# Two DVE operations of 512 columns in an edge loop, each made as two of 256

## The reference

```python
edge_attr = swish(edge_attr_raw @ enc_W + enc_b)
for _ in range(4):
    e_in = concatenate([edge_attr, x[src], x[dst]], axis=-1)
    e_upd = layernorm(swish(e_in @ eW1 + eb1) @ eW2 + eb2, eg, ebeta)
    edge_attr = edge_attr + e_upd
    agg = segment_sum(edge_attr, dst, 3125)
    n_in = concatenate([x, agg], axis=-1)
    x = x + layernorm(swish(n_in @ nW1 + nb1) @ nW2 + nb2, ng, nbeta)
```

## Time and profile before

| | |
|---|---|
| three runs | 3330.44, 3335.55 (median), 3336.2 us |
| the profiled execution | 3340.0 us, its span 3338.2 us |
| busy share of the span | PE 78%, DVE 70%, ACT 62%, POOL 51% |
| mean granted TensorE clock | 0.944 of full speed |

### The profile page before, as it was taken

One profiled execution on the slowest core, in us unless ns is written; L12 is line 12 of the kernel. 1 busy time (PEld: TensorE's weight loads), 2 busy tenths in 40 slices (PEclk: granted clock), 3 DMA queues, 4 the chain that ended last, 5 costly groups with the idle time before them and its releaser, 6 DMA issues.

```text
span 3338.2 us, 86010 instructions
## 1 busy us (share of the span) xinstructions
PE 2607.4 (78%) x28086; PEld 1912.4 (57%) x28086; DVE 2346.5 (70%) x6798; ACT 2072.7 (62%) x5534; POOL 1707.8 (51%) x1679
## 2 busy tenths in 40 slices
PE   3665888888886788888887788888888688888885
PEld 1332666666663566666664566666665466666664
DVE  6884677777784577777775477777776377777778
ACT  3774666666663666666664566666664466666672
POOL 1445565656522555555530656665640656666640
PEclk8666999999998999999998899999999799999998
DMA  4776566666644566666653566666653455555540
GB/s 129 247 240 211 171 197 195 196 199 196 194 138 130 164 197 193 196 197 193 195 159 114 155 199 195 203 195 197 198 168 112 143 156 160 157 161 157 163 135 23
DMA packets 492917, 578.04 MB, mean 173 GB/s; under 512 B 82399, under 2 KB 341724, under 8 KB 492446
## 3 DMA queue, kind: packets, MB, share of 16 engines
q1 hardware_dynamic: 417198, 366.82, 34.6%
q0 software_dynamic: 75264, 205.62, 23.0%
HBM read 428.62 MB, written 144.35 MB: 172 GB/s over the span
## 4 chain that ended last, share of the span: by engine, by line
PE 54%; issue 17%; ACT 10%; DVE 7%; another core or an unknown queue 6%; DMA 3%; SPq 1%; DVEq 1%; ACTq 0%; POOL 0%; POOLq 0%
PE psum L1137 12%; PE psum L1153 12%; PE psum L1129 11%; PE psum L1121 4%; PE psum L1101 4%; PE psum L1169 4%; ACT arena L1267 3%; ACT arena L1255 3%; ACT psum L1241 2%; DMA arena<-attr_p 2%; PE psum L1148 2%; PE psum L1566 2%; PE psum L1605 1%; ACT arena L1281 1%
## 5 line engine op out<-in xcount | busy, mean ns | idle before, releaser
L1078 POOL DMA_INDIRECT arena<-node_tables,idx_all x1568 | 1587.2, 1012 | 1354.5 <-PE psum L1129 617.0
L1255 ACT ACTIVATE arena<-psum 128x128 f32<-128x128 f32 x1568 | 411.7, 278 | 744.5 <-remote 726.8
L1129 PE MATMUL psum<-ident,arena 128*128 128x128 f16 x6272 | 547.1, 220 | 400.2 <-issue 394.6
L1129 PEld LDWEIGHTS psum<-ident,arena 128*128 128x128 f16 x6272 | 398.1, 98 | 530.0 <-issue 515.9
L1345 DVE SCALAR_TENSOR_TENSOR arena<-psum,arena 128x1024 f16<-128x1024 f32 x392 | 477.2, 1217 | 205.2 <-issue 120.7
L1153 PE MATMUL psum<-w_hi,arena 128*128 128x128 f16 x6272 | 593.8, 220 | 4.4 <-DVE arena L1345 3.8
L1153 PE MATMUL psum<-w_lo,arena 128*128 128x128 f16 x3136 | 549.1, 220 | 0.5 <-issue 0.5
L1415 DVE TENSOR_TENSOR agg<-agg,psum 128x128 f32 x392 | 113.1, 289 | 578.9 <-remote 556.4
L1137 PE MATMUL psum<-arena,w_hi 128*128 128x512 f16 x1568 | 482.8, 389 | 32.9 <-issue 32.9
L1240 ACT ACTIVATE arena<-psum 128x1024 f16<-128x1024 f32 x392 | 402.6, 1027 | 169.2 <-issue 89.7
L1153 PEld LDWEIGHTS psum<-w_hi,arena 128*128 128x128 f16 x6272 | 501.3, 98 | 5.9 <-DVE arena L1345 4.9
(11 more groups left out here) (171 smaller groups left out, 3519.7 us busy)
## 6 DMA issues: line engine op xcount, KB each, us to landing
state<-arena SPq DMA_DIRECT2D x392, 256.0 KB, 3.9
arena<-state SPq DMA_DIRECT2D x392, 256.0 KB
arena<-matrices SPq DMA_DIRECT2D x784, 64.0 KB
arena<-node_tables SPq DMA_DIRECT2D x784, 64.0 KB
node_tables<-arena SPq DMA_DIRECT2D x100, 256.0 KB, 2.5
arena<-node_tables,idx_all POOLq DMA_INDIRECT x1568
arena<-rel_rows SPq DMA_DIRECT2D x98, 128.0 KB, 4.0
matrices<-arena SPq DMA_DIRECT2D x98, 128.0 KB, 3.7
```

What stands on the lines that cost most here:

```text
L1078: pool.indirect_dma_start(out=rows[k][:, t, :], out_offset=None, in_=p_table, in_offset=bass.IndirectOffsetOnAxis(ap=idx_all[:, g, t:t + 1 ...
L1129: x = pe.matmul(ps_h(k2)[:, half, t * P:(t + 1) * P], rows[k][:, t, p * H + half * D:p * H + half * D + D], ident16[:, :], start=False, st ...
L1255: x = act.activation(sq[k2][:, t * P:(t + 1) * P], ps_v(k2)[:, t * P:(t + 1) * P], ACT.Square, accum_out=nv[pair][:, n:n + 1])
```

## The change

DVE's `add_old` and `low_new` each issue two operations over two of the four tiles (256 columns) in place of one over all four (512 columns). The waits ahead of them are as before, and the semaphore is raised by the second operation alone.

```diff
                     dve.wait_ge(S("scaled"), c(i, off))
                     e3 = e_new[k].rearrange("p (t f) -> p t f", t=TPG)
-                    dve.scalar_tensor_tensor(e3, e3, 1.0, st_in[k8][:, :, 0:D], ALU.mult, ALU.add).then_inc(S("new"), 1)
+                    for pair in (slice(0, 2), slice(2, 4)):
+                        x = dve.scalar_tensor_tensor(e3[:, pair, :], e3[:, pair, :], 1.0, st_in[k8][:, pair, 0:D], ALU.mult, ALU.add)
+                    x.then_inc(S("new"), 1)
...
                     dve.wait_ge(S("eh"), c(i, off))
-                    dve.scalar_tensor_tensor(st_out[k][:, :, D:2 * D], e_new[k].rearrange("p (t f) -> p t f", t=TPG), 1.0,
-                                             st_out[k][:, :, 0:D], ALU.mult, ALU.subtract).then_inc(S("el"), 1)
+                    for pair in (slice(0, 2), slice(2, 4)):
+                        x = dve.scalar_tensor_tensor(st_out[k][:, pair, D:2 * D], e_new[k].rearrange("p (t f) -> p t f", t=TPG)[:, pair, :],
+                                                     1.0, st_out[k][:, pair, 0:D], ALU.mult, ALU.subtract)
+                    x.then_inc(S("el"), 1)
```

## The result

The changed kernel took 3361.61 us (median of four runs, 3360.4 to 3365.74), the kernel before 3333.67 us (four runs, 3330.44 to 3336.2): ratio 1.0085, interval 1.0069 to 1.0101. It is 28 us slower. The forecast was 3338.2 us, within 0.2% of no change, with a range up to 3351.

A forecast was written before the change was run, and what follows sets the result against it. The prediction took PE's work plus a stop of unknown cause, not DVE, to bound each 6.81 us period. It added 0.9 + 1.0 + 0.7 = 2.6 us to the median 3335.55, giving 3338.2 us, range 3330 to 3351.

The forecast's parts named there:

- The price of the operations: On DVE, each split operation costs 0.067 us more, a group 0.133 us, all 392 groups 52 us of DVE's time.
- The estimate of 47 us: Slowdown by the skill page's fixed 0.060 us, were it paid on the path in all 784 places.
- Step ends: At the four steps' ends, 0.9 us for 13 places on the chain and 0.7 us where DVE's spare time runs out.
- The other 1.0 us of the forecast: In the middle of the steps, the chain that ended last holds the two changed lines 15 times, at 0.067 us each.
- The step that failed: In 334 groups, DVE's added 0.133 us only shortens its wait of 1.55 to 1.77 us before the addition; cost 0.
- if the wait before L1415 stays at its length while the periods grow: Sign of being wrong, at DVE's wait before its addition, expected to fall from 556 to about 512 us.
- the stop's ends are at a fixed distance from PE's work: In PE's stop, 2.98 and 2.95 us from its last output matmul; no part of the 6.81 us period waits for DVE.
- Passes through everywhere: Rival: the stop ends after something of DVE, each group grows by 0.133 us, the kernel by 52 us to 3388; chance 0.06.
- More of the groups are exposed: Rival: more groups pay DVE's added time, or the price doubles; 7.7 to 15.3 us more, 3343 to 3351; chance 0.15.
- Faster: Rival: breaks in DVE's operations shorten POOL's gathers; a tenth of 113 us excess gives 11 us, 3324; chance 0.11.

The follow-up runs named there:

- i: The kernel before, with the eight transposes of the state on PE made six times over; 3518.17 us.
- j: The changed kernel, with the eight transposes of the state on PE made six times over; 3520.02 us.
- l: The kernel before, with only the sum with the old high part (`add_old`) in four operations of 128 columns; 3347.18 us, 1.0065, with the stop.
- m: The kernel before, with only the new low part (`low_new`) in four operations of 128 columns; 3350.35 us, 1.0071, with the stop.
- h2: The changed kernel run again, in a batch with the stop, against the kernel before; 3357.13 us, 1.0096.
- c_split4: The kernel before, with both `add_old` and `low_new` in four operations of 128 columns, in a batch without the stop; 2803.15 us, 1.0189.

## Why the prediction was wrong

**The price of the operations: right.** 0.067 us for each split operation, against a median of 0.069 in three places of four (in the fourth, `add_old` in even slots, about nothing); 421 ns against 422 forecast, and 0.67 us for two halves against 0.667. The fixed cost that the Trainium skill names ("VectorE: DVE Perf Modes", section on the TRN2 errata, 58 cycles at 0.96 GHz) is borne out too: 0.060 us against 0.069. The estimate of 47 us that the prediction worked out from it is far off with the stop, where 28 to 31 us were lost, and without it, where nothing was.

**Step ends: too dear.** 0.9 + 0.7 = 1.6 us for the ends of the steps; measured were 1.0 us in the last five groups of the loops and -0.7 us outside the loops. The other 1.0 us of the forecast, for places in the middle of the loops, can't be told apart from the rest of the loss.

**The step that failed** is "In the 334 groups in which DVE stands before L1415, it shortens that wait ... Nothing queued behind it moves. Cost: 0." It failed twice.

*The wait.* It doesn't get shorter: 1.67 us each time before and after, 543.0 us in all and not 512. The changed operations stand behind the addition, and the wait that they reach first is the one before L1345. That one has room in the kernel with long PE work, and there it took up the whole change (54.3 us between i and j). With the stop it has little: in the kernel before, in the groups with the usual stop, DVE waits 0.25 us before L1345 in one parity of the groups and not at all in the other, so 0.133 us more in each group can't all be taken up there. The prediction had named this sign itself: "if the wait before L1415 stays at its length while the periods grow". It would have read it as a stop that follows DVE, which the steady 3.0 us speaks against.

*The cost.* Behind the step stood the sentence that the stop's ends are at a fixed distance from PE's work and not from anything DVE does. The distance did stay, 2.98 to 2.99 us. But I took the length of the stop for all that it costs, and it isn't: PE gets a few matmuls of the next group through during the stop, and those that don't get through are paid for behind it. In the changed kernel 1.5 fewer of 16 got through, 0.08 us, in each of some 290 groups, and the ordinary period grew by 0.059 us where nothing was forecast. The number of matmuls behind the stop stood in the very rows that I quoted (11 and 9), and I had not asked what sets it.

**The rivals.** "Passes through everywhere" had the right sign and named the right weak point, the stop, but its price of 52 us was nearly twice the loss, and proportionality to DVE's time is refuted by l and m. "More of the groups are exposed" ended at 3351, ten short of the measured time. "Faster" held that POOL's gathers are shortened when DVE's long operations are broken up, and that the stop might end by POOL. The first half is seen: the mean gather fell from 1012 to 1004 ns, though the kernel got slower. The second doesn't fit the usual stop: in the changed kernel's 288 groups with one of 2.8 to 3.2 us its end varies by 0.035 us (standard deviation) against PE's last output matmul and by 0.09 us against POOL's fourth gather. Only in the 20 groups with a stop of over 3.6 us is the end steadier against POOL, 0.06 us.

**What stays open.** What the stop is, and why it comes in some batches and not in others. In batches without it, more instructions on SP or on PE didn't bring it on. Why the change lowers the number of matmuls that pass during it isn't shown either; counts and time of DVE's operations both fail to give the sizes of h2, l and m. One lead is in the traces. In the kernel before, halve the ordinary groups by the time of the four gathers under way as the stop begins: in the half with the shorter ones, 4.86 us in the mean, 10.4 matmuls remain, in the half with the longer ones, 5.09 us, 6.6. In even groups splitting both operations went with shorter gathers, 4.94 to 4.88 us, and with more matmuls behind the stop, 7.5 to 10.1; in odd groups both hardly moved (5.01 us and 5.01, 9.5 and 9.8). So DVE's work may reach PE's stop by way of POOL. That is a correlation; within the changed kernel the two halves are alike (10.0 and 9.8), and no run varied the gathers alone with the stop present.

## What to carry to other kernels

Added work is taken up first by the next wait behind it in the engine's own list, so it is that wait's length that counts, and not that of the engine's longest wait. An idle time whose releaser the profile can't name is no room to hide work in until an experiment has shown that it is. When a periodic stop is found, ask what passes during it as well as how long it lasts. And a split or a reordering on DVE is to be judged by what it does to POOL's gathers too, once these take part in the bound.

## What the runs showed of the hardware

- The same program takes 2751 to 2763 us or 3326 to 3334 us, depending on the batch; one chip showed both. The difference goes with a stop of PE of 3.0 us in most groups. ACT's squares and DVE's addition, which wait for semaphores that PE raises, start only at its end: in the changed kernel PE's last output matmul starts at 1507.46, and L1255 on ACT starts at 1510.57 after a wait of 1.98 us with no named releaser.
- An operation of DVE over 128 columns that reads no scalar operand takes 0.202 us from start to start (c_split4), 0.069 us on top of its columns at 1.04 ns; the scale operation of the same shape, which reads a scalar for each partition, takes 0.263 us in the same trace, 0.130 us on top.
- Operations of DVE over 72 columns in place of 8, eleven for each two groups, lengthened POOL's indirect gathers from 1003 to 1132 ns in the mean.
- Empty instructions in ACT's or DVE's list left both the recorded instructions (86010) and the bytes of the instruction queues as they were.
